# Last expert stage of a decoder block on one core: four result buffers, a first expert by single chunks, and three drains of GpSimd

## The chip, the cores and the metric

The program runs on one core of one Trainium2 chip. The metric is the device time of one execution, in microseconds. The core has five engines with instruction streams of their own: TensorE (PE; its weight loads are PEld), VectorE (DVE), ScalarE (ACT), GpSimd (POOL) and SyncE (SP), and 16 DMA engines. Engines wait for each other by semaphores; each executes its own stream in order.

## The reference

Two gated residual pairs over x of 32 x 128 tokens with 256 columns, all in float32:

```python
x = x + tanh(g_xattn[0]) * _L0_xattn_ref(_layernorm(x), ctx, ctx, mask, ...)  # 16 heads of 16
x = x + tanh(g_ffn[0])   * _L0_ffn_ref(_layernorm(x), ...)    # 8 experts, each takes its best 512 tokens
x = x + tanh(g_xattn[1]) * _L1_xattn_ref(_layernorm(x), ctx, ...)
x = x + tanh(g_ffn[1])   * _L1_ffn_ref(_layernorm(x), wg, W, b)
```

The change is mostly in the last line, a feed-forward in which each token goes to its first choice of 8 experts, and each expert takes its first 512 tokens:

```python
probs = softmax(xt @ wg); idx = argmax(probs)
mask = one_hot(idx, 8); locations = cumsum(mask, axis=0) - mask
mask = mask * (locations < 512)
gate = sum(probs * mask)
exp_out = einsum('ech,efh->ecf', exp_in, W) + b[:, None, :]
out = einsum('tec,ecf->tf', gate * dispatch, exp_out)
```

## The kernel before

The program has two blocks, each closed by a barrier of all engines: the front (layer norm and attention of the first pair) and `behind_attention` (L2262 on), in which five stages stand one behind the other in each engine's stream: routing, expert choice, the second attention (`bidirectional_stage`, L1504), and the last expert stage (`first_choice_stage`, L2117). Semaphores alone order the stages, so an engine that has finished its part of one begins with the next. On leaving the program a context clears all semaphores and passes a second barrier (L48, L49).

GpSimd issues all indirect DMAs, each of 128 rows: 32 that gather rows for expert choice (L1357), 32 that add its results (L1366), 32 that scatter the rows of the second attention into `slots` (L1651), ordered by expert, and 32 that scatter the results of the last stage into the output (L2161).

In the second attention's stream on GpSimd (`on_gpsimd`, loop over steps s from -2 to 10, L1643) a step has the inverse deviation of quad s - 2 of the result, the four slot scatters of quad s - 3, and the inverse deviation of the input of quad s + 2. A quad is 4 tiles of 128 tokens; there are 8. The last two steps with work give GpSimd eight scatters without a pause between them.

The last stage works expert by expert (8), each of 512 slots in four chunks of 128:

- SyncE (`on_sync`, L2144) waits for all 32 slot scatters, and then loads expert 0's rows in two halves (L2151) and those of experts 1 to 3 whole (L2153). The weights of experts 0 to 3 were loaded earlier. Weights, bias and rows of expert e from 4 on are loaded when all results of expert e - 4 are there (L2136).
- VectorE (`on_vector`) has `norm(e)`, four instructions that normalise an expert's chunks into `xn` (L2183); `index(e)`, which makes the target indices `idx` (L2189) and from expert 2 on waits until the scatters of expert e - 2 have landed, since `y` and `idx` have two buffers each (L2188); `chunk(e, c)`, bias (L2197) and gated residual (L2192) of one chunk; and `pair(e, j)`, bias of two chunks in one instruction (L2203) and two results. Its order is norm 0, index 0, norm 1, chunks 0 and 1 of expert 0, norm 2, pair (0, 1), index 1, pair (1, 0), norm 3, pair (1, 1), index 2, and so on.
- TensorE (`on_tensor`) turns two chunks at a time (`turn`, four transposes by the identity, L2231) and multiplies them by the weights (`pair`, eight matmuls, L2245), two matmuls a chunk.
- ScalarE copies each turned pair from PSUM to `rT` (L2173).
- GpSimd (`on_gpsimd`, L2155) waits for the stores of the attention, then issues for each expert four scatters, each behind its result (L2160), and at the end waits until all have landed (L2165).

The order of VectorE's stream is written out by hand:

```python
        norm(0)
        index(0)
        norm(1)
        for e in range(EXPERTS):
            if e == 0:
                chunk(0, 0)
                chunk(0, 1)
            else:
                pair(e, 0)
            if e + 2 < EXPERTS:
                norm(e + 2)
            pair(e, 1)
            if e + 1 < EXPERTS:
                index(e + 1)
```

## Time and profile before

| | |
|---|---|
| median of 3 runs | 802.15 us (800.67 to 803.16) |
| the profiled execution | 800.73 us |
| its span, first to last instruction | 798.9 us |
| mean granted clock of TensorE | 0.936 of full speed |
| busy: PE, DVE, ACT, POOL | 85%, 54%, 39%, 33% |

Times in a trace are microseconds from the start of the span; those marked ns are nanoseconds. In a timeline a row is a run of like instructions: start, length, engine, line, operation, output<-inputs, shapes, count, and in brackets the engine's idle time before it with what ended it. `POOLq`, `SPq` and the like are instructions of an engine's sequencer, such as a DRAIN or a wait for a semaphore. Ends of matmuls are modelled. The granted clock is given as a share of TensorE's full speed: 1.00 is 2.4 GHz, 0.50 is 1.2 GHz. A scatter's instruction on GpSimd ends when the DMA has been issued, not when it has landed.

### The profile page before, as it was taken

The numbers are of one execution on the slowest core, as the hardware profiler recorded it, in microseconds if no ns is written. First come the engines' busy times: TensorE is split into PE (matmuls) and PEld (weight loads), VectorE is DVE, ScalarE is ACT, GpSimd is POOL, SyncE is SP. The second block draws the span as 40 slices with busy tenths as digits, with TensorE's granted clock in tenths as the row PEclk, the third lists the DMA queues.
The fourth block names the chain that finished last, engine by engine and source line by source line (L and its number), as shares of the span: only waits on it lengthen the run. The fifth ranks groups of instructions, "written<-read, shape, count | busy, mean of one in ns | idle before, by whom it ended". The sixth has DMA issues, their size and how long they took to land.

```text
span 798.9 us, 14703 instructions
## 1 busy us (share of the span) xinstructions
PE 675.1 (85%) x5289; PEld 462.4 (58%) x5289; DVE 433.6 (54%) x1317; ACT 315.1 (39%) x673; POOL 260.3 (33%) x377
## 2 busy tenths in 40 slices
PE   5999998999999975847999999995799999982980
PEld 3565655555555543623666666664677778761860
DVE  5645546777787746782222222103567776772781
ACT  2343434777777762532222222222554444301220
POOL 4101102244334422005555555221113332224563
PEclk9999997999999997966999999997899999996995
DMA  8569924466676118912363893216233451113651
GB/s 269 186 180 253 257 101 96 91 135 135 129 132 128 57 55 200 171 40 83 50 155 48 256 260 75 47 21 196 80 106 133 140 179 50 59 53 129 208 168 53
DMA packets 105039, 103.10 MB, mean 129 GB/s; under 512 B 22102, under 2 KB 95321, under 8 KB 104964
## 3 DMA queue, kind: packets, MB, share of 16 engines
q1 hardware_dynamic: 95752, 85.72, 41.2%
q0 software_dynamic: 9216, 16.46, 9.2%
q8 instruction: 42, 0.69, 0.4%
q14 instruction: 29, 0.24, 0.1%
HBM read 60.15 MB, written 42.25 MB: 128 GB/s over the span
## 4 chain that ended last, share of the span: by engine, by line
PE 35%; DVE 7%; issue 6%; ACT 4%; POOL 4%; DMA 3%; another core or an unknown queue 1%; SPq 0%; POOLq 0%; DVEq 0%; ACTq 0%
PE pc L1486 9%; PE pc L1463 9%; PE pc L950 3%; POOL result L2161 2%; PE pc L2029 2%; ACT enc L1851 2%; PE pc L1991 1%; PE pc L1988 1%; PE pc L1482 1%; PE pc L2051 1%; DVE d_w_c L1772 1%; PE pc L1466 1%; PE pc L1959 1%; PE pc L1450 1%
## 5 line engine op out<-in xcount | busy, mean ns | idle before, releaser
L617 ACT ACTIVATE probs<-pb,b_key_cols 128x512 f32<-128x512 f32 x128 | 92.7, 779 | 16.6 <-PE pb L787 16.6
L484 DVE TENSOR_REDUCE neg_max<-pb 128x4 f32<-128x512 f32 x128 | 81.7, 680 | 3.5 <-PE pb L767 3.5
L1366 POOL DMA_INDIRECT scratch_resid<-y,k_idx x32 | 54.7, 1708 | 87.3 <-DVE y L1416 87.0
L1463 PE MATMUL pc<-gT,w_up 128*128 128x512 f32 x160 | 72.6, 610 | 0.9 <-DVE gT L1398 0.9
L1486 PE MATMUL pc<-w_dn,mid 128*128 128x256 f32 x320 | 73.3, 384 | 0.0
L1434 ACT ACTIVATE mid<-pc,b_up 128x512 f32<-128x512 f32 x40 | 27.5, 687 | 113.4 <-PE pc L1463 111.4
L1486 PEld LDWEIGHTS pc<-w_dn,mid 128*128 128x128 f32 x320 | 59.5, 190 | 12.7 <-issue 5.3
L1463 PEld LDWEIGHTS pc<-gT,w_up 128*128 128x128 f32 x160 | 31.3, 196 | 37.7 <-issue 37.3
L1416 DVE TENSOR_SCALAR y<-pc,gate 128x256 f32<-128x256 f32 x32 | 15.5, 484 | 65.7 <-PE pc L1486 47.9
L1357 POOL DMA_INDIRECT rows<-scratch_rows,k_idx x32 | 31.1, 973 | 56.8 <-DVE k_idx L1240 47.4
L365 POOL CAST nm_parts<-neg_max 128x16 bf16<-128x16 f32 x32 | 6.3, 196 | 124.9 <-DVE neg_max L484 124.9
L800 PE MATMUL pb<-probs,v_wide 128*32 128x128 f32 x1024 | 42.5, 285 | 1.8 <-ACT probs L617 1.8
L863 PE MATMUL pb<-wo,attnT 128*128 128x264 f32 x128 | 37.6, 417 | 5.1 <-ACT attnT L664 0.9
L1398 DVE COPY gT<-pc 128x512 f32<-128x512 f32 x8 | 5.5, 692 | 65.9 <-PE pc L1450 65.1
L2161 POOL DMA_INDIRECT result<-g_y,g_idx x32 | 31.8, 992 | 24.5 <-DVE g_y L2192 14.5
L502 DVE SCALAR_TENSOR_TENSOR s_x<-pb,s_tanh_g,s_x 128x264 f32<-128x264 f32 x32 | 15.8, 493 | 41.7 <-PE pb L863 41.7
L1651 POOL DMA_INDIRECT scratch_slots<-s_x,r_dest x32 | 32.5, 1016 | 9.4 <-issue 9.4
L1991 PE MATMUL pc<-d_w_c,encT 128*128 128x256 f32 x128 | 33.9, 388 | 0.0
L1988 PE MATMUL pc<-k_w_f,ehqT 128*128 128x256 f32 x128 | 33.5, 385 | 0.0
L787 PE MATMUL pb<-qs,ks 51*128 51x128 bf16 x512 | 26.0, 223 | 8.4 <-ACT probs L617 8.4
L691 PE MATMUL pb<-cT,wk 128*128 128x512 f32 x64 | 32.1, 645 | 1.3 <-ACT cT L584 1.3
L1639 POOL TENSOR_TENSOR d_vareps<-d_moments,s_eps 128x4 f32<-128x4 f32 x8 | 1.6, 197 | 94.0 <-DVE d_moments L1735 94.0
(336 smaller groups left out, 1443.1 us busy)
## 6 DMA issues: line engine op xcount, KB each, us to landing
qs<-scratch_qparts SPq DMA_DIRECT2D x48, 128.0 KB, 4.3
ks<-scratch_kparts SPq DMA_DIRECT2D x48, 128.0 KB
w_dn<-in_W_down SPq DMA_DIRECT2D x8, 640.0 KB
scratch_slots<-s_zero SPq DMA_DIRECT2D x1, 4160.0 KB, 19.1
c_in<-in_ctx SPq DMA_DIRECT2D x8, 512.0 KB, 6.5
s_x<-in_x SPq DMA_DIRECT2D x8, 512.0 KB, 7.0
scratch_ctxT<-cT SPq DMA_DIRECT2D x8, 512.0 KB, 6.5
scratch_resid<-s_x SPq DMA_DIRECT2D x16, 256.0 KB, 3.1
```

The lines of the kernel that those rows point to most:

```text
L484: V.tensor_reduce(neg_max[:, h:h + 4], ps_s[b][:].rearrange("p (h k) -> p h k", h=4), AX.X, ALU.max, negate=True).then_inc(max_s, 1)
L617: A.activation(probs[2 * u + b][:], ps_st[b][:].rearrange("p (h q) -> p h q", h=4), ACT.Exp, bias=key_cols[:, 1, t:t + 1], scale=key_cols[ ...
L691: ins = M.matmul(ps_ck[m][:], wk[:, h, m * P:(m + 1) * P], cT[q % 2][:, h, :], start=(h == 0), stop=(h == HALVES - 1))
L800: ins = M.matmul(ps_ctx[32 * j:32 * j + SLOTW, g * P:(g + 1) * P], v_wide[t % 2][:, 4 * g + j, :], probs[2 * u + b][:, j, :], start=True, ...
L863: ins = M.matmul(ps_o, attnT[:, h, :], wo[:, h, :], start=(h == 0), stop=(h == HALVES - 1))
L1366: pool.indirect_dma_start(out=T["resid"], out_offset=bass.IndirectOffsetOnAxis(ap=S["idx"][:, e, c:c + 1], axis=0), in_=y[e % 2][:, c, :], ...
L1463: ins = nc.tensor.matmul(ps_u[k % 4][:], w, gT[e % 2][:, h, :], start=(h == 0), stop=(h == HALVES - 1))
L1486: ins = nc.tensor.matmul(here(c), mid[e % 2][m][:, c * P:(c + 1) * P], w_dn[e % 2][:, m, :], start=False, stop=(m == MT - 2))
L1651: pool.indirect_dma_start(out=T["slots"], out_offset=bass.IndirectOffsetOnAxis(ap=dest[:, t, :], axis=0), in_=rows[:, t, :], in_offset=Non ...
L1988: M.matmul(here, ehqT[q % 2][:, h, cols], w_f[:, 2, h, :], start=False, stop=False)
L1991: ins = M.matmul(here, encT[q % 2][:, h, cols], w_c[q % 2][:, t, h, :], start=False, stop=(h == HALVES - 1))
L2161: pool.indirect_dma_start(out=T["out"], out_offset=bass.IndirectOffsetOnAxis(ap=idx[e % 2][:, c:c + 1], axis=0), in_=y[e % 2][:, c, :], in ...
```

## The change

In the second attention GpSimd gets a `drain()` at step 1. In the last stage:

- `y`, `idx` and the semaphores `sent` have four buffers instead of two, and `index(e)` waits for scatters from expert 4 on, for those of expert e - 4.
- Expert 0's rows are loaded as chunk 0 and then chunks 1 to 3. It is turned, copied and multiplied chunk by chunk, each chunk in a PSUM bank of its own. VectorE's order becomes norm 0, index 0, chunks 0 and 1, norm 1, chunks 2 and 3, norm 2, index 1, and then from expert 1 on as before.
- TensorE waits for all slot scatters and turns the identity 14 times ahead of chunk 0.
- GpSimd drains at the start of the stage and once behind the last scatter, ahead of the waits for the landings.

```diff
--- before.py
+++ after.py
@@ -1653,6 +1653,8 @@
                                             bounds_check=TOKENS - 1, oob_is_err=False).then_inc(sent_s, 16)
             if is_quad(s + 2):
                 inverse_deviation(s + 2)
+            if s == 1:
+                pool.drain()
 
     def tables_on_vector(dve):
         V = nc.vector
@@ -2116,16 +2118,18 @@
 
 def first_choice_stage(nc, S, T, sem, sb, ps, bidir):
 
-    ST = CAP // P
+    ST, WARM = CAP // P, 14
     two = lambda n, s, d=F32: [sb(f"{n}{i}", s, d) for i in range(2)]
     rows, xn = [sb(f"g_rows{i}", [P, ST, ROW1]) for i in range(4)], [sb(f"g_xn{i}", [P, ST, D]) for i in range(3)]
     rT = two("g_rT", [P, HALVES, CAP])
     w, bias = S["w_1"], S["b_1"]
-    yb, y, idx = two("g_yb", [P, ST, D]), two("g_y", [P, ST, D]), two("g_idx", [P, ST], I32)
-    sent = [sem(f"pg_sent{i}") for i in range(2)]
+    yb = two("g_yb", [P, ST, D])
+    y, idx = [sb(f"g_y{i}", [P, ST, D]) for i in range(4)], [sb(f"g_idx{i}", [P, ST], I32) for i in range(4)]
+    sent = [sem(f"pg_sent{i}") for i in range(4)]
     in_s = [sem(f"pg_in{i}") for i in range(4)]
-    half_s = sem("pg_half")
-    place = lambda e, c: ps[6 if (e, c) == (0, 1) else 4 + e % 2 * 2 + c // 2][:, c % 2 * D:(c % 2 + 1) * D]
+    rest_s = sem("pg_rest")
+    place = lambda e, c: ps[(4, 6, 5, 7)[c] if e == 0 else 4 + e % 2 * 2 + c // 2][:, c % 2 * D:(c % 2 + 1) * D]
+    turned = lambda e, j: ST + 2 * (e - 1) + j + 1
     xn_s, t_ps, rT_s, y_ps, yb_s, y_s, idx_s = (sem("pg_" + n) for n in ("xn", "t_ps", "rT", "y_ps", "yb", "y", "idx"))
     slots_t = T["slots"].rearrange("(c p) d -> p c d", p=P)
 
@@ -2147,27 +2151,33 @@
             if e >= 4:
                 weights(sp, e)
             if e == 0:
-                for j in range(2):
-                    sp.dma_start(rows[0][:, 2 * j:2 * j + 2, :], slots_t[:, 2 * j:2 * j + 2, :]).then_inc((in_s[0], half_s)[j], 16)
+                sp.dma_start(rows[0][:, 0:1, :], slots_t[:, 0:1, :]).then_inc(in_s[0], 16)
+                sp.dma_start(rows[0][:, 1:ST, :], slots_t[:, 1:ST, :]).then_inc(rest_s, 16)
             else:
                 sp.dma_start(rows[e % 4][:], slots_t[:, e * ST:(e + 1) * ST, :]).then_inc(in_s[e % 4], 16)
 
     def on_gpsimd(pool):
+        pool.drain()
         pool.wait_ge(bidir.stored_s, 16 * QUADS)
         for e in range(EXPERTS):
             pool.wait_ge(idx_s, e + 1)
             for c in range(ST):
                 pool.wait_ge(y_s, e * ST + c + 1)
-                pool.indirect_dma_start(out=T["out"], out_offset=bass.IndirectOffsetOnAxis(ap=idx[e % 2][:, c:c + 1], axis=0),
-                                        in_=y[e % 2][:, c, :], in_offset=None,
-                                        bounds_check=TOKENS - 1, oob_is_err=False).then_inc(sent[e % 2], 16)
-        for par in range(2):
-            pool.wait_ge(sent[par], 16 * ST * EXPERTS // 2)
+                pool.indirect_dma_start(out=T["out"], out_offset=bass.IndirectOffsetOnAxis(ap=idx[e % 4][:, c:c + 1], axis=0),
+                                        in_=y[e % 4][:, c, :], in_offset=None,
+                                        bounds_check=TOKENS - 1, oob_is_err=False).then_inc(sent[e % 4], 16)
+        pool.drain()
+        for i in range(4):
+            pool.wait_ge(sent[i], 16 * ST * EXPERTS // 4)
 
     def on_scalar(act):
-        for e in range(EXPERTS):
+        for c in range(ST):
+            act.wait_ge(t_ps, c + 1)
+            nc.scalar.activation(rT[0][:, :, c * P:(c + 1) * P], ps[c][:, 0:D].rearrange("p (h t) -> p h t", h=HALVES),
+                                 ACT.Copy).then_inc(rT_s, 1)
+        for e in range(1, EXPERTS):
             for j in range(2):
-                act.wait_ge(t_ps, 2 * e + j + 1)
+                act.wait_ge(t_ps, turned(e, j))
                 if e >= 2:
                     act.wait_ge(y_ps, (e - 2) * ST + 2 * j + 2)
                 nc.scalar.activation(rT[e % 2][:, :, 2 * j * P:2 * (j + 1) * P], ps[e % 2 * 2 + j][:].rearrange("p (h t) -> p h t", h=HALVES),
@@ -2176,20 +2186,21 @@
     def on_vector(dve):
         def norm(e):
             if e >= 3:
-                dve.wait_ge(t_ps, 2 * (e - 2))
+                dve.wait_ge(t_ps, ST if e == 3 else turned(e - 3, 1))
+            dve.wait_ge(in_s[e % 4], 48 * (e // 4 + 1))
             for c in range(ST):
-                if c % 2 == 0:
-                    dve.wait_ge(half_s if e == 0 and c else in_s[e % 4], 16 if e == 0 and c else 48 * (e // 4 + 1))
+                if (e, c) == (0, 1):
+                    dve.wait_ge(rest_s, 16)
                 nc.vector.tensor_scalar(xn[e % 3][:, c, :], rows[e % 4][:, c, 0:D], rows[e % 4][:, c, D:D + 1], rows[e % 4][:, c, D + 1:D + 2],
                                         ALU.subtract, ALU.mult).then_inc(xn_s, 1)
 
         def index(e):
-            if e >= 2:
-                dve.wait_ge(sent[e % 2], 16 * (e // 2) * ST)
-            nc.vector.tensor_scalar(idx[e % 2][:], rows[e % 4][:, :, D + 3], -1.0, float(TOKENS), ALU.mult, ALU.add).then_inc(idx_s, 1)
+            if e >= 4:
+                dve.wait_ge(sent[e % 4], 16 * (e // 4) * ST)
+            nc.vector.tensor_scalar(idx[e % 4][:], rows[e % 4][:, :, D + 3], -1.0, float(TOKENS), ALU.mult, ALU.add).then_inc(idx_s, 1)
 
         def result(e, c):
-            nc.vector.scalar_tensor_tensor(y[e % 2][:, c, :], yb[e % 2][:, c, :], rows[e % 4][:, c, D + 2:D + 3],
+            nc.vector.scalar_tensor_tensor(y[e % 4][:, c, :], yb[e % 2][:, c, :], rows[e % 4][:, c, D + 2:D + 3],
                                            rows[e % 4][:, c, 0:D], ALU.mult, ALU.add).then_inc(y_s, 1)
 
         def chunk(e, c):
@@ -2208,13 +2219,15 @@
 
         norm(0)
         index(0)
+        chunk(0, 0)
+        chunk(0, 1)
         norm(1)
-        for e in range(EXPERTS):
-            if e == 0:
-                chunk(0, 0)
-                chunk(0, 1)
-            else:
-                pair(e, 0)
+        chunk(0, 2)
+        chunk(0, 3)
+        norm(2)
+        index(1)
+        for e in range(1, EXPERTS):
+            pair(e, 0)
             if e + 2 < EXPERTS:
                 norm(e + 2)
             pair(e, 1)
@@ -2222,10 +2235,27 @@
                 index(e + 1)
 
     def on_tensor(pe):
+        def turn_chunk(c):
+            pe.wait_ge(xn_s, c + 1)
+            for h in range(HALVES):
+                ins = nc.tensor.transpose(ps[c][:, h * P:(h + 1) * P], xn[0][:, c, h * P:(h + 1) * P], S["ident"][:])
+            ins.then_inc(t_ps, 1)
+
+        def product(e, c):
+            for h in range(HALVES):
+                ins = nc.tensor.matmul(place(e, c), rT[e % 2][:, h, c * P:(c + 1) * P],
+                                       w[e % 4][:, h, :], start=(h == 0), stop=(h == HALVES - 1))
+            ins.then_inc(y_ps, 1)
+
+        def product_of_first(c):
+            pe.wait_ge(rT_s, c + 1)
+            if c == 0:
+                pe.wait_ge(in_s[0], 48)
+            product(0, c)
+
         def turn(e, j):
             pe.wait_ge(xn_s, e * ST + 2 * j + 2)
-            if e >= 2:
-                pe.wait_ge(rT_s, 2 * (e - 2) + j + 1)
+            pe.wait_ge(rT_s, 2 + j + 1 if e == 1 else 2 * j + 2 if e == 2 else turned(e - 2, j))
             for h in range(HALVES):
                 for c in (2 * j, 2 * j + 1):
                     ins = nc.tensor.transpose(ps[e % 2 * 2 + j][:, (2 * h + c % 2) * P:(2 * h + c % 2 + 1) * P], xn[e % 3][:, c, h * P:(h + 1) * P],
@@ -2233,22 +2263,30 @@
             ins.then_inc(t_ps, 1)
 
         def pair(e, j):
-            pe.wait_ge(rT_s, 2 * e + j + 1)
+            pe.wait_ge(rT_s, turned(e, j))
             if j == 0:
                 pe.wait_ge(in_s[e % 4], 48 * (e // 4 + 1))
             if e >= 2:
                 pe.wait_ge(yb_s, (e - 2) * ST + 2 * j + 2)
-            if (e, j) == (1, 0):
-                pe.wait_ge(yb_s, 2)
+            if e == 1:
+                pe.wait_ge(yb_s, 2 * j + 2)
             for c in (2 * j, 2 * j + 1):
-                for h in range(HALVES):
-                    ins = nc.tensor.matmul(place(e, c), rT[e % 2][:, h, c * P:(c + 1) * P],
-                                           w[e % 4][:, h, :], start=(h == 0), stop=(h == HALVES - 1))
-                ins.then_inc(y_ps, 1)
-
-        turn(0, 0)
-        turn(0, 1)
-        for e in range(EXPERTS):
+                product(e, c)
+
+        pe.wait_ge(bidir.sent_s, 16 * TILES)
+        for _ in range(WARM):
+            nc.tensor.transpose(ps[7][:, 0:P], S["ident"][:], S["ident"][:])
+        turn_chunk(0)
+        turn_chunk(1)
+        product_of_first(0)
+        turn_chunk(2)
+        product_of_first(1)
+        turn_chunk(3)
+        product_of_first(2)
+        turn(1, 0)
+        product_of_first(3)
+        turn(1, 1)
+        for e in range(1, EXPERTS):
             pair(e, 0)
             if e + 1 < EXPERTS:
                 turn(e + 1, 0)
```

## Rows read from the trace of the kernel before

**Rows 1.** The page: chain by line, and two groups (busy us, mean ns, idle).
```profile
PE pc L1486 9%; PE pc L1463 9%; PE pc L950 3%; POOL result L2161 2%; PE pc L2029 2%; ACT enc L1851 2%; PE pc L1991 1%; PE pc L1988 1%; PE pc L1482 1%; PE pc L2051 1%; DVE d_w_c L1772 1%; PE pc L1466 1%; PE pc L1959 1%; PE pc L1450 1%
...
L1366 POOL DMA_INDIRECT scratch_resid<-y,k_idx x32 | 54.7, 1708 | 87.3 <-DVE y L1416 87.0
...
L1357 POOL DMA_INDIRECT rows<-scratch_rows,k_idx x32 | 31.1, 973 | 56.8 <-DVE k_idx L1240 47.4
```

**Rows 2.** Line 2161's instructions (ns min/median/max, first to last start), and who waited.
```profile
L2161 POOL DMA_INDIRECT result<-g_y,g_idx x32: 971/973/1142, 742.8 to 787.4; - x32
...
  DVE g_idx L2189: 7.7, 5
```

**Rows 3.** Timeline of POOL, last stage.
```profile
744.09 0.97 POOL L2161 DMA_INDIRECT result<-g_y,g_idx  x1 [0.30 <-issue]
746.13 0.97 POOL L2161 DMA_INDIRECT result<-g_y,g_idx  x1 [1.07 <-DVE g_y L2192]
...
752.70 0.97 POOL L2161 DMA_INDIRECT result<-g_y,g_idx  x1 [0.31 <-issue]
754.74 1.03 POOL L2161 DMA_INDIRECT result<-g_y,g_idx  x1 [1.06 <-issue]
...
773.10 1.03 POOL L2161 DMA_INDIRECT result<-g_y,g_idx  x1 [0.67 <-issue]
```

**Rows 4.** Timeline of DVE, in expert 2.
```profile
752.67 0.69 DVE L2203 TENSOR_TENSOR g_yb<-pc,b 128x512 f32<-128x512 f32 x1
...
754.19 1.38 DVE L2183 TENSOR_SCALAR g_xn<-g_rows 128x256 f32<-128x256 f32 x4
```

**Rows 5.** Timeline of all engines, head of the last stage.
```profile
733.48 0.88 SPq L2151 DMA_DIRECT2D g_rows<-scratch_slots  x2
...
736.16 1.46 DVE L2183 TENSOR_SCALAR g_xn<-g_rows 128x256 f32<-128x256 f32 x4 [9.67 <-DMA g_rows<-scratch_slots]
...
736.95 1.97 PE L2231 MATMUL pc<-s_ident,g_xn 128*128 128x128 f32 x8 [12.09 <-DVE g_xn L2183]
...
739.65 1.38 DVE L2183 TENSOR_SCALAR g_xn<-g_rows 128x256 f32<-128x256 f32 x4 [1.95 <-DMA g_rows<-scratch_slots]
740.94 0.42 DVE L2197 TENSOR_TENSOR g_yb<-pc,b 128x256 f32<-128x256 f32 x1
741.40 0.48 DVE L2192 SCALAR_TENSOR_TENSOR g_y<-g_yb,g_rows 128x256 f32<-128x256 f32 x1
```

**Rows 6.** Instructions of lines 2165 and 2264, tail of the program.
```profile
L2165 POOLq EVENT_SEMAPHORE  x1: 17/17/17, 789.8 to 789.8; - x1
...
L2264 POOLq DRAIN  x1: 7162/7162/7162, 790.0 to 790.0; - x1
```

**Rows 7.** Instructions of lines 49 and 48, POOL's other drains.
```profile
L49 POOLq DRAIN  x2: 45/46/46, 305.9 to 798.6; - x2
...
L48 POOLq DRAIN  x2: 184/235/286, 305.2 to 797.4; - x2
```

**Rows 8.** Timeline of POOL, second attention.
```profile
593.14 0.20 POOL L1639 TENSOR_TENSOR d_vareps<-d_moments,s_eps 128x4 f32<-128x4 f32 x1 [13.81 <-DVE d_moments L1735]
```

**Rows 9.** Instructions of line 1651.
```profile
L1651 POOL DMA_INDIRECT scratch_slots<-s_x,r_dest x32: 971/976/1283, 612.5 to 731.1; - x32
```

**Rows 10.** Lines 2231 and 2245, from 736.9 to 740.6 us and from 742 to 750.
```profile
L2231 PE MATMUL pc<-s_ident,g_xn x8: 421/421/476, 737.0 to 738.5; 128*128 128x128 f32 x8
...
L2245 PE MATMUL pc<-w,g_rT x4: 634/634/793, 738.8 to 740.2; 128*128 128x256 f32 x4
...
L2245 PE MATMUL pc<-w,g_rT x31: 379/379/382, 742.1 to 749.9; 128*128 128x256 f32 x31
```

**Rows 11.** Groups by form, an ACT copy of 256 columns.
```profile
L664 ACT ACTIVATE attnT<-pb 128x256 f32<-128x256 f32 x32 | 12.3, 383 | 39.3 <-PE pb L891 39.3
```

**Rows 12.** Windows: stretch, length, busy of PE, PEld, DVE, ACT, POOL, then PEclk.
```profile
736.95:740.93 3.98, 3.98 (x13) 3.38 (x14) 2.03 (x7) 1.19 (x2) 0.00 (x0) 0.50 1.02 341
740.94:752.70 11.76, 11.76 (x67) 10.33 (x67) 9.24 (x25) 2.99 (x5) 7.00 (x7) 1.00 0.54 157
```

## The prediction

> **What bounds the kernel now.** I read the page first, for its chain of waits and its groups; then GpSimd's instructions and timeline in the last stage; then the two ends of that stage, because the edits sit there. The page's chain is spread thinly over many lines, with GpSimd's result scatters (L2161) the only line of the last stage in it [rows 1]. Their own view says why: 32 scatters, the first starts at 742.8 and the last at 787.4 [rows 2]. Where they are queued, from 773.10 to 787.4, eleven steps take 14.3 us, 1.30 each [rows 2, 3]. 31 such steps would be 40.3 us and the stage takes 44.6, so 4.3 us are holes. They have two kinds: at the start (744.09 to 746.13, one step too long by 0.7) and about once per expert later (752.70 to 754.74) [rows 3]. The view of the line names the second kind: VectorE's index waited 7.7 us, in five pieces, for landed scatters [rows 2], which is the wait for one of two result buffers. Without it VectorE would need 1.52 us for a pair (752.67 to 754.19), 1.38 for normalising, 1.52 for the second pair and under 0.2 for the index, 4.6 an expert [rows 4], against 4 x 1.30 = 5.2 on GpSimd. So the stage's floor is GpSimd issuing, once it is fed.
>
> At the head of the stage SyncE issues the loads at 733.48, and VectorE waits until 739.65 to normalise expert 1 before it takes expert 0's first product at 740.94 [rows 5]. At the tail the last scatter starts at 787.4, its landing is seen at 789.8, and then one DRAIN of GpSimd takes 7.16 us, from 790.0 [rows 2, 6]. Everything after it is 798.9 less 797.2, 1.7 us.
>
> **The drains.** GpSimd's drains of two other lines took 0.05 to 0.29 us, at 305 behind the front part and at 797 right behind the long one [rows 7]. The long one differs in what preceded it: 128 indirect DMAs (four groups of 32, at L1357, L1366, L1651 and L2161) since the drains at 305, none before the short ones [rows 1, 2, 9]. All had landed, so it isn't a wait for data. I read it as settling something per DMA: 7.16 / 128 = 0.056 us each. The trace doesn't show a drain after fewer DMAs; its bounds are 0.05 (a drain after none) and 7.16 (after all), and by the backlog of 32 DMAs I take 1.8.
> - Drain at s == 1: it stands behind GpSimd's work for quad 3; the next instruction is at 593.14, after 13.8 us of idle time [rows 8]. 64 DMAs make 3.6 us, even 7.16 fits. Queued behind it is only that next instruction, so it costs nothing.
> - Drain at the start of the last stage: GpSimd's last slots scatter starts at 731.1 and takes 1.0 [rows 9], its next work comes at about 740 (below). 32 DMAs, 1.8 us; 7.16 would end at 739.3, still hidden. Waiting behind it would be the first result scatter.
> - Drain behind the last scatter: it starts 1.0 after that scatter's start and ends at 2.8; the landing comes at 2.4 and hides all but 0.4. Then 0.24 as now from landing to drain, the last drain at about 0.2, and 1.7: 4.9 us from the last start to the end, where it is 798.9 - 787.4 = 11.5 now. **Saved: 6.6.** Ends: 7.0 if the third is short (the landing then decides), 1.2 if it takes 7.16 itself, 0 if the last keeps its 7.16.
>
> Now a rule against this. The row shows 7162 ns [rows 6]. The Trainium skill, page "VectorE: DVE Perf Modes", section "The DRAIN you can't avoid", says of the drains that frame a kernel that they are a constant of about 12 ns on all five engines. By it neither an early nor a late drain could be worth anything; this trace doesn't agree: even GpSimd's shortest take 45 ns, and I go by the row.
>
> **The head of the stage.** SyncE now loads chunk 0 alone (a quarter instead of a half) and the other three together. Today the half reaches VectorE 2.68 us after the issue at 733.48 [rows 5]; the bytes halved are worth at most that share of it that is transfer, and I take 0.35: VectorE at 735.8, its first 0.41 us done at 736.2. The rest lands as the second half does now, about 736.9. TensorE runs 14 turned identities from 733.5 on. At the lower clock turns start 0.21 apart ((1.97 - 0.42) / 7 = 0.22 at most) and last 0.42 [rows 5, 10], so they end at 736.5: they hold chunk 0's turns back 0.3 us. Then: turns of chunk 0 to 737.15; ScalarE's copy of 256 columns, 0.38 us by a like copy [rows 11], to 737.6; TensorE turns chunk 1 meanwhile (its normalised rows are there at 737.3) to 737.8; product of chunk 0.
> What clock has that product? Now it is 0.50 until 740.93, four microseconds after TensorE began at 736.95 [rows 12]. It will have begun at 733.5 and be nearly unbroken, so I put the rise at about 737.5. Two matmuls then take 0.6 (379 ns, 0.22 apart) instead of 1.1 (634 ns, 0.43 apart) [rows 10]: product at 738.3, or 738.9 if the clock stays low.
> VectorE: rest of expert 0 normalised and index by 738.05; chunk 0 at 738.3, 0.94 for bias and result (740.94 to 741.88) [rows 5]; GpSimd 0.9 later, at **740.1** instead of 742.8. Chunk 1 follows to 740.15 (expert 1's rows are in at 739.65 as now); normalising expert 1 to 741.4; chunks 2 and 3, results at 742.35 and 743.25; normalising expert 2 (now behind all chunks of expert 0) to 744.5; index; pair (1,0), results at 745.8 and 746.2; normalising expert 3, pair (1,1) first result at 748.65. GpSimd, 1.30 a step or result plus 0.85: 740.1, 741.4, 743.2, 744.5, then a hole, 746.65, 747.95, 749.5 for the seventh. From there VectorE (4.6) outruns GpSimd (5.2). Four buffers make the index of expert e wait for scatters of e - 4, which VectorE's lead of at most 4 us never reaches, so no hole comes back. Loads of experts 4 to 7 are let go by the results of four experts before, a little earlier than now; they are needed over 6 us later, and the first load took 2.7. TensorE does 24 instructions an expert and did 67 in the 11.76 us of the stretch in which it never paused [rows 12], 4.2 us an expert, less than 5.2.
> Last scatter: 749.5 + 25 x 1.30 = 782.0. **Saved: 5.4** of 787.4. With the low clock until 741 every step is 0.6 to 1 us later: 4.4. Ends: 3.0 if, beside the low clock, a later landing of chunk 1 and VectorE's work before pair (1,0) make the holes 1.4 longer, and 7.6 with no hole at all (740.1 + 31 x 1.28 = 779.8).
>
> **Sum.** 5.4 + 6.6 = 12.0: span 786.9. The profiled execution took 800.73 (span 798.9), the median of the runs is 802.15; I take the difference off the median: **790.2 us**.
>
> **Rivals.** A difference of 0.3%, 2.4 us, is about what a measurement of this kernel can tell from none.
> - *The clock stays low until 741* (TensorE pauses about 0.4 us before chunk 1): 5.4 becomes 4.4, 791.2. For it: the rise came late before as well. Against: hardly a gap is left. Chance 0.14.
> - *A drain costs 7.16 whenever any indirect DMA stands before it.* The first two stay hidden, the third doesn't: 1.2 instead of 6.6, 795.6. For it: no trace shows a middle value. Against: 7.16 is odd as a flat fee beside 0.05. 0.08.
> - *The 7.16 belong to the end of the block, whatever was drained earlier.* Then the change's drains don't do what they should: 802.15 - 5.4 = 796.8. This is also where the page's rule would leave it, with drains of no weight in themselves; the rows give it little, 0.07.
> - *Slower: a drain with transfers in flight waits far longer than one that finds all landed.* The second and third drains both stand right behind scatters. At price D the second holds GpSimd until 732.1 + D, and 31 steps lead to 772.4 + D; the third adds D again: the span ends at 775.5 + 2D. It decides from D = 11.7 us on; with D = 14.3 (twice the 7.16) the span is 804.1, the time 807.4. Against: the scatters land 1.4 us after their end. 0.03.
>
> **How the numbers follow.** Forecast 0.62 (790.2); the four rivals 0.32; 0.06 for a mixture that leaves about no gain or something not seen. The low end is the forecast with no hole at the head, 802.15 - 14.2 = 788.0; the high end takes in the flat fee, 796.0. Left out are the third rival (0.07), the slower one (0.03), most of the 0.06 and a little below the low end: about 0.2. Faster by over 0.3%: 0.62 + 0.14 + 0.08 + 0.07 and a little, 0.92; within 0.3%: 0.05; slower 0.03.
>
> **What would show it.** Drains of GpSimd of about 3.6, 1.8, 1.8 and 0.2 us; the first result scatter at about 740; one hole before the fifth, none of over 0.3 us after the seventh; no wait of VectorE for a landed scatter; the clock at 1.0 from about 737.5. Wrong it would be by a third drain near 7 us, a last drain near 7 us, a first scatter after 741.5, or steps between scatters of over 1.35 on average.

## The result, and the profile after

The changed kernel took 798.33 us (median of 8 runs, 795.73 to 800.41), the kernel before 801.2 us beside it (8 runs, 800.19 to 805.91): ratio 0.995, 95% interval 0.993 to 0.9971. It is faster, by 2.9 us between the medians where 12.0 were forecast; 798.3 lies outside the forecast range of 788 to 796. The profiled execution took 796.69 us, its span is 794.9 us (before 800.73 and 798.9), the mean granted clock 0.944 (0.936).

The page of the changed kernel, the group of the result scatters:

```profile
L2166 POOL DMA_INDIRECT result<-g_y,g_idx x32 | 32.1, 1002 | 26.1 <-DVE g_y L2203 19.0
```

The same line by its instructions (ns min/median/max, first to last start; then what ended its idle time):

```profile
L2166 POOL DMA_INDIRECT result<-g_y,g_idx x32: 972/976/1202, 740.8 to 789.0; - x32
its engine sat idle before it (us, times) until:
  DVE g_y L2203: 19.0, 9
  issue: 7.2, 23
```

Beside [rows 2]: the first scatter comes 2.0 us earlier (740.8, was 742.8), the last 1.6 us *later* (789.0, was 787.4). No wait of the index for landed scatters is left. So the last stage lost more than its head won; what remains of the gain is behind the last scatter: 794.9 - 789.0 = 5.9 us, where it was 11.5. The new drains, and the one that closes the block (views of four lines, the same columns):

```profile
L1657 POOLq DRAIN  x1: 6470/6470/6470, 577.8 to 577.8; - x1
...
L2160 POOLq DRAIN  x1: 6223/6223/6223, 728.4 to 728.4; - x1
...
L2169 POOLq DRAIN  x1: 5069/5069/5069, 787.7 to 787.7; - x1
...
L2302 POOLq DRAIN  x1: 55/55/55, 793.1 to 793.1; - x1
```

A drain's record here begins while the scatters ahead of it are still being issued (the third at 787.7, the last scatter at 789.0), so its length says little; its end does. The third ends at 787.70 + 5.07 = 792.77, 2.8 us after the last issue's end (789.99). The one that cost 7.16 us in [rows 6] takes 0.055.

The timeline of the head, beside [rows 5]:

```profile
733.28 3.25 PE L2278 MATMUL pc<-s_ident 128*128 128x128 f32 x14 [8.65 <-DMA scratch_slots<-s_x,r_dest]
...
735.47 0.41 DVE L2194 TENSOR_SCALAR g_xn<-g_rows 128x256 f32<-128x256 f32 x1 [9.22 <-DMA g_rows<-scratch_slots]
...
737.00 0.38 ACT L2176 ACTIVATE g_rT<-pc 128x256 f32<-128x256 f32 x1 [13.47 <-PE pc L2241]
737.11 1.06 DVE L2194 TENSOR_SCALAR g_xn<-g_rows 128x256 f32<-128x256 f32 x3 [1.23 <-DMA g_rows<-scratch_slots]
...
737.85 1.03 PE L2246 MATMUL pc<-w,g_rT 128*128 128x256 f32 x4
...
738.92 0.42 DVE L2208 TENSOR_TENSOR g_yb<-pc,b 128x256 f32<-128x256 f32 x1 [0.67 <-PE pc L2246]
...
740.80 0.99 POOL L2166 DMA_INDIRECT result<-g_y,g_idx  x1 [8.97 <-DVE g_y L2203]
```

Windows of the same kernel (columns as in [rows 12]):

```profile
733.28:736.40 3.12, 3.12 (x15) 3.12 (x16) 0.41 (x1) 0.00 (x0) 0.00 (x0) 0.50 0.66 163
737.06:751.00 13.94, 12.82 (x71) 11.05 (x72) 12.71 (x35) 4.46 (x9) 6.83 (x7) 1.00 0.69 220
```

The head is what was forecast, clock included. A chunk's product is two matmuls in the code and four in the profile, 1.03 us. The stage goes wrong later. The timeline of all engines in experts 3 and 4:

```profile
753.84 0.60 PE L2261 MATMUL pc<-s_ident,g_xn 128*128 128x128 f32 x4
...
754.28 1.89 PE L2246 MATMUL pc<-w,g_rT 128*128 128x256 f32 x8
...
756.01 0.60 PE L2261 MATMUL pc<-s_ident,g_xn 128*128 128x128 f32 x4
...
758.28 0.60 ACT L2183 ACTIVATE g_rT<-pc 128x512 f32<-128x512 f32 x1 [5.37 <-remote]
758.93 1.59 PEld L2246 LDWEIGHTS pc<-w,g_rT 128*128 128x128 f32 x8 [2.56 <-issue]
...
759.35 0.97 POOL L2166 DMA_INDIRECT result<-g_y,g_idx  x1 [0.31 <-issue]
...
761.91 0.69 DVE L2214 TENSOR_TENSOR g_yb<-pc,b 128x512 f32<-128x512 f32 x1 [4.02 <-PE pc L2246]
...
763.92 0.97 POOL L2166 DMA_INDIRECT result<-g_y,g_idx  x1 [3.59 <-DVE g_y L2203]
```

TensorE's turns for expert 4 are recorded at 753.84 and over by 754.44. ScalarE, which waits for them (and for a product of expert 2 that VectorE had read long before), copies them at 758.28. The product for the second half of expert 3 is recorded at 754.28 and over by 756.17; VectorE, idle for 4.0 us, takes it at 761.91, and GpSimd, which needs the result, has a hole of 3.6 us. These are two late completions of TensorE beside each other: the product did not wait for the late copy. A second hole, of 3.1 us, lies before the scatter at 782.45. A lower clock did not cause them: windows of one microsecond show 1.00 from 751 to 781. It fell to 0.50 at the end of the second hole, ahead of the last product. In the view of waits, from 730 us on, the same shows as waits ended by "remote", for which the trace has no recorded instruction that ended them:

```profile
POOL result L2166 <- DVE g_y L2203: 19.0, 9, 9.0
ACT g_rT L2183 <- remote: 15.7, 3, 5.4
...
ACT g_rT L2183 <- PE pc L2261: 10.9, 6, 3.0
...
DVE g_yb L2214 <- remote: 5.9, 1, 5.9
```

(columns: engine and line, what it waited for, us in total, times, longest). I call it "late completions of TensorE" below. The word "remote" marks only part of them: the wait of 4.0 us above is put down to TensorE. The kernel before has it too, and I had not read it: its waits from 740 to 800 us hold

```profile
ACT g_rT L2173 <- remote: 7.8, 3, 3.2
```

### The profile page after: what moved, and what is told of

Same layout as the page of the kernel before. It is cut to its first block, busy times and chain, and to the rows that moved or that the text cites. A ratio compares the mean times of both kernels' runs of the same rounds, so it can differ in the third digit from the quotient of the medians.

```text
span 794.9 us, 14740 instructions
## 1 busy us (share of the span) xinstructions
PE 676.6 (85%) x5303; PEld 464.4 (58%) x5303; DVE 433.9 (55%) x1318; ACT 315.6 (40%) x675; POOL 261.0 (33%) x377
## 4 chain that ended last, share of the span: by engine, by line
PE 38%; DVE 9%; issue 4%; ACT 4%; DMA 3%; another core or an unknown queue 2%; POOL 1%; POOLq 0%; SPq 0%; DVEq 0%; ACTq 0%
PE pc L1486 9%; PE pc L1463 9%; PE pc L950 3%; PE pc L2246 2%; PE pc L2031 2%; PE pc L1990 1%; ACT enc L1853 1%; PE pc L1993 1%; PE pc L1482 1%; DVE d_w_c L1774 1%; PE pc L2053 1%; PE pc L1466 1%; DVE d_stats L1745 1%; PE pc L1450 1%
## 5 line engine op out<-in xcount | busy, mean ns | idle before, releaser
L1366 POOL DMA_INDIRECT scratch_resid<-y,k_idx x32 | 54.7, 1709 | 87.0 <-DVE y L1416 86.7
L2246 PE MATMUL pc<-w,g_rT 128*128 128x256 f32 x128 | 32.5, 396 | 9.6 <-ACT g_rT L2183 4.9
```

The source lines that it names most:

```text
L1366: pool.indirect_dma_start(out=T["resid"], out_offset=bass.IndirectOffsetOnAxis(ap=S["idx"][:, e, c:c + 1], axis=0), in_=y[e % 2][:, c, :], ...
L2246: ins = nc.tensor.matmul(place(e, c), rT[e % 2][:, h, c * P:(c + 1) * P], w[e % 4][:, h, :], start=(h == 0), stop=(h == HALVES - 1))
```

## The experiments

Eighteen runs of eleven kernels follow. The kernel before took 791.3 us beside the first four; beside all others 801.7 to 805.8 (801.2 beside the timing above), in one case on the very chip that had given 791.3. No run shows what differed. I call them the short and the long condition. Each ratio is to the kernel before beside it.

### The two parts alone, short condition

drains_only is the kernel before with the three drains; no_drains is the changed kernel without them.

```diff
+            if s == 1:
+                pool.drain()
...
     def on_gpsimd(pool):
+        pool.drain()
...
+        pool.drain()
         for par in range(2):
```

> The kernel before with the three drains alone. Theory A (the drains carry the whole gain, the rest of the change nothing): the last scatter starts where it does before, about 787.4, and the tail behind it shrinks from 11.5 to about 5.9 us as in the changed kernel, so about 795.6 us, ratio 0.993. Theory B (the drains and the head of the stage both gain, and something else took 6 us back by chance of that run): the same tail, but the changed kernel is then clearly faster than this one. The third drain should take about 2.8 us from the end of the last scatter's instruction.

> The changed kernel without its three drains, so with the four buffers, the single chunks and the turned identities alone. Theory A (late completions of TensorE eat what the head and the buffers bring): last scatter between 786 and 790, one last drain of about 7 us, 800 to 804 us. Theory B (they bring what was forecast, 5.4 us, and the profiled execution was unlucky): 795 to 797 us.

drains_only: ratio 0.9923 (0.9897 to 0.9949), about 6.1 us of 791.3, 5.8 us from the last scatter to the end. no_drains: 0.9954 (0.9935 to 0.9972), 3.6 us. From SyncE's load of the rows to the last scatter, which is free of what comes earlier, drains_only takes 776.7 - 723.0 = 53.7 us and no_drains 774.3 - 724.2 = 50.1: also 3.6. The stage without drains:

```profile
L2163 POOL DMA_INDIRECT result<-g_y,g_idx x32: 972/975/1212, 731.7 to 774.3; - x32
```

One hole ahead of the fifth scatter and no other, no wait ended by "remote" in the stage, and a turned pair reaches ScalarE at once (744.79 + 0.60 = 745.39):

```profile
744.79 0.60 PE L2257 MATMUL pc<-s_ident,g_xn 128*128 128x128 f32 x4
...
745.42 0.60 ACT L2179 ACTIVATE g_rT<-pc 128x512 f32<-128x512 f32 x1 [1.57 <-PE pc L2257]
```

So in the short condition both parts work: together 9.7 us by the two ratios, if they add (the whole was not timed there), where 12.0 were forecast. The times expected for these two runs were for the long condition and can't be compared.

### The same in the long condition

after_again, after_third and after_fourth are the changed kernel, before_again the kernel before, drains_only_again and no_drains_again the kernels above. For after_third, too, 0.992 to 0.995 was expected where the kernel before takes about 802 us.

> The changed kernel once more, now beside its parts. The kernel before took 791 us where the parts were run and 801 where the changed kernel was first timed, and only in the first traces do TensorE's completions arrive late (up to 6 us). Theory A (the late completions belong to the chip or its condition, and cost the changed kernel more than the one before, because its last stage leans on TensorE without a pause): where the kernel before takes about 791, this one is at 0.987 to 0.989 of it, with the last scatter 50 us behind the first load and no lag above 0.5 us; where the kernel before takes about 801, it is at 0.995 again with two holes of about 3 us. Theory B (the parts don't add up anywhere): 0.992 to 0.995 in either place.

> The kernel before, for its trace in the same place as the trace of the changed kernel. Theory A: at a time of about 791 its trace has no lag of TensorE's completions, and last scatter starts 53 to 54 us behind the first load; at about 801 it has lags in the second attention and in the last stage.

> The kernel before with the three drains alone, beside the changed kernel. Theory A: at 802 the two are equal within 1 us, since the late completions take back what the head and the buffers give; at 791 the changed kernel is faster by 3 to 4 us. Theory B: equal in both places.

> The changed kernel without the three drains, that is the head and the four buffers alone. It had 0.9954 where the kernel before takes 791 us. Where the kernel before takes some 802 us: Theory A, the unbroken issuing gives back what head and buffers gain: two holes of 3 to 5 us, 47 to 49 us from first to last scatter, ratio 0.998 to 1.002. Theory B, head and buffers gain their part wherever they run, and the drains are worth less there: ratio 0.994 to 0.997.

| kernel | ratio (95%) | first scatter to last, us | rows' load to last scatter |
|---|---|---|---|
| before, the two profiles | | 44.6, 45.6 | 53.9, 55.7 |
| after_again | 0.9924 (0.9897 to 0.9951) | 49.1 | 56.6 |
| after_third | 0.994 (0.9921 to 0.9959) | 48.7 | 56.1 |
| after_fourth | 0.9922 (0.9894 to 0.995) | 47.1 | 54.7 |
| drains_only_again | 0.9934 (0.9909 to 0.996) | 45.4 | 55.2 |
| no_drains_again | 1.0 (0.9979 to 1.0021) | 49.1 | 57.1 |
| no_third_drain (below) | 0.9929 (0.9906 to 0.9952) | 46.4 | 53.9 |
| no_first_drain (below) | 0.9939 (0.9918 to 0.996) | 47.5 | 55.1 |

As far as these times can tell, the drains are the whole gain: 0.9934 alone, and 0.9934 is also the mean of the changed kernel's four ratios (0.995, 0.9924, 0.994, 0.9922; the first timing was its worst). Head and buffers alone give nothing, within 1.7 us either way, where the short condition had 3.6. All kernels of the table with the head reach their first scatter 7.5 to 8.0 us after the load, the kernel before after 9.3 and 10.1. In this condition all nine profiles with four buffers and no pauses have two steps of 2.9 to 5.0 us; the five in which the index still waits for landings (head_two_waits below among them) have none or one, of up to 4.3. So two buffers have holes too, but fewer. before_again has late completions too (two waits of ScalarE ended by "remote", 8.1 us) and one step of 4.3.

Where the long condition begins shows in no_drains and no_drains_again, the same kernel on the same chip. Their first slots scatters start at 613.1 and 613.6 us, their last ones at 721.8 and 730.8: 8.5 of the 16.0 us between the two spans arise in the second attention, 7.1 in the last stage.

### What a drain costs

no_third_drain is the changed kernel without the drain behind the last scatter, no_first_drain without the one at s == 1.

> The changed kernel without its third drain alone. Theory C (a drain first waits for the landing, about 1.4 us behind the end of the last issue, and then settles each indirect DMA since the drain before at 0.043 us): the last drain, from behind the landing, takes 1.4 us, and the time is that of the changed kernel within 0.3 us: the third drain hides nothing. Theory D (a drain settles at 0.08 us a DMA from the end of the last issue on, beside the landing): the last drain takes 2.6 to 2.8 us and the kernel is 1.2 us slower.

> The changed kernel without the drain at step 1 of the second attention, so that the one at the start of the last stage finds 96 indirect DMAs instead of 32. It ends 2.75 us after the last issue in the changed kernel. By a price per DMA it ends 6.8 to 8.1 us after the last issue, at or after the first result scatter is due (8.9 us after it), so the time stays within 0.3 us; by a flat price it stays at 2.75.

The drain lines of no_drains, no_third_drain, no_first_drain and no_scatter (below), in this order:

```profile
L2298 POOLq DRAIN  x1: 7162/7162/7162, 777.0 to 777.0; - x1
```

```profile
L2301 POOLq DRAIN  x1: 2660/2660/2660, 792.1 to 792.1; - x1
```

```profile
L2158 POOLq DRAIN  x1: 9707/9707/9707, 731.8 to 731.8; - x1
```

```profile
L2171 POOLq DRAIN  x1: 4642/4642/4642, 765.6 to 765.6; - x1
```

The first two stand behind the landed data and so show the price pure: 7.16 us after 128 indirect DMAs, 2.66 after 32. The third stands behind 96 and ends 6.2 us after the last slots scatter's issue (735.29 to 741.53), the fourth behind 8, 1.8 us after the last issue (768.40 to 770.20). The drain at s == 1 in the changed kernel, behind 64, ends 5.3 us after GpSimd's last instruction. 8, 32, 64, 96, 128 DMAs: 1.8, 2.7, 5.3, 6.2, 7.2 us. It grows with the DMAs since the last drain, but not at 0.056 each. Two expectations missed here: 8 were expected to take under 1 us, and 96 from 6.8 to 8.1 us. The 64 are gathers and additions, the 8 and 32 are scatters; whether the kind counts beside the number, no run tells.

no_third_drain: 0.9929 (0.9906 to 0.9952), 7.1 us from last scatter to end instead of 5.9: the drain beside the landing hides 1.2 us, and the other two do most of the work. no_first_drain: 0.9939 (0.9918 to 0.996); its drain of 96 ends 2.8 us before the first result scatter (744.31) and is still hidden. By the ratios neither can be told from the whole change.

### Issuing, or moving rows?

no_scatter leaves out the result scatters of experts 1 to 6; out_of_range gives those experts indices beyond the output, so that GpSimd issues them and no row is moved. In no_scatter the waits for the scatters that are left out go too. Each ran once in either condition.

```diff
                 pool.wait_ge(y_s, e * ST + c + 1)
+                if 1 <= e <= 6:
+                    continue
```

```diff
-... -1.0, float(TOKENS), ALU.mult, ALU.add)
+... -1.0, float(TOKENS if e in (0, 7) else 3 * TOKENS), ALU.mult, ALU.add)
```

> The changed kernel, with the scatters of experts 1 to 6 left out (their rows don't reach the output). Theory A (TensorE's completions arrive late because GpSimd issues scatters without a pause): no lag of a completion above 0.5 us in the last stage, and VectorE finishes expert 7 at about 776 to 778, set by TensorE and VectorE's 4.3 to 4.6 us an expert. Theory B (TensorE's completions are late whatever GpSimd does): two delays of 3 to 6 us stay, at about 755 to 762 and 775 to 781. The last drain, after 8 DMAs, should be under 1 us by a price per DMA.

> The changed kernel, with the target indices of experts 1 to 6 out of range, so that GpSimd issues all 32 scatters but 24 of them move no rows (those rows are not written). If the issuing itself makes TensorE's completions late, the holes of 3 us stay as in the changed kernel, last scatter near 789. If the data that the scatters move make them late, they are gone, and the last scatter starts near 782 to 783.

> The changed kernel, with the scatters of experts 1 to 6 left out (their rows don't reach the output). At 802: if GpSimd's scatters make TensorE's completions late (theory P), the lags in the second attention stay, where its scatters are still issued, and those of the last stage are gone, with the first of the remaining scatters of expert 7 at 32 to 33 us behind that of expert 0, as it was at 791. If TensorE is late by itself in its busiest stretches (theory T), lags of 1 us and more stay in the last stage and this distance is 36 us or more.

> The changed kernel, with the target indices of experts 1 to 6 out of range, so that 24 of 32 scatters move no rows (those rows are not written). At 802: if the moving of rows makes the completions late, no lag in the last stage and about 42.6 us from the first to the last scatter, as it was at 791; if the issuing does, or TensorE itself, lags of over 1 us stay and the distance is 47 us or more.

Short condition: 774.28 and 779.74 us; out_of_range takes 42.7 us from first to last scatter, as no_drains does with its rows moved (42.6). Without the scatters expert 7's first comes 32.7 us after expert 0's first: 32.7 / 7 = 4.7 us an expert, by my estimate what VectorE needs, under the 4 x 1.32 of GpSimd. Long condition: 779.97 and 797.21 us. The waits from 740 to 780 us, first without the scatters, then with scatters that move nothing:

```profile
POOL result L2168 <- DVE g_y L2205: 28.4, 2, 28.1
ACT g_rT L2185 <- PE pc L2263: 17.6, 11, 1.8
ACT g_rT L2185 <- PE pc L2248: 1.6, 1, 1.6
```

```profile
ACT g_rT L2183 <- PE pc L2261: 18.6, 8, 4.7
POOL result L2166 <- DVE g_y L2203: 15.3, 7, 8.9
...
ACT g_rT L2183 <- remote: 6.5, 1, 6.5
...
DVE g_yb L2214 <- remote: 4.2, 1, 4.2
```

Without scatters no completion is late in the last stage, and it takes 33.6 us instead of 32.7. With issued but empty ones they are late, and the holes are steps of 4.4 and 5.0 us. In the second attention, where both kernels issue the slots scatters, both keep theirs, and in the short condition there are none at all. So in the last stage the lateness goes with GpSimd issuing scatters, not with rows moved; this rests on one profile of each kernel. Issuing alone is not enough: in the expert choice, from 358 to 540 us, GpSimd issues 64 indirect DMAs, 32 of them gathers and 32 additions, and none of the 20 profiles has a wait ended by "remote" before its first slots scatter. In all 16 of the long condition the first such wait ends 3.5 to 4.2 us after that scatter's start (615.63 against 612.10 in the changed kernel's profile).

### Which part opens the holes?

head_two_waits keeps the change but makes the index of expert e wait for the scatters of e - 2, as with two buffers. drains_buffers is the kernel before with the drains and four buffers and its old head. pool_pause is the changed kernel with a memset on GpSimd behind each of the first seven experts.

```diff
         def index(e):
-            if e >= 4:
-                dve.wait_ge(sent[e % 4], 16 * (e // 4) * ST)
+            if e >= 2:
+                dve.wait_ge(sent[(e - 2) % 4], 16 * ((e - 2) // 4 + 1) * ST)
```

```diff
+    pause = sb("g_pause", [P, EXPERTS - 1, 1024])
...
+            if e < EXPERTS - 1:
+                nc.gpsimd.memset(pause[:, e, :], 0.0)
```

> The changed kernel once more, beside the three variants below. The theory that both parts of the change add (0.9923 for the drains and 0.9954 for the head and buffers, where the kernel before took 791 us) has, where the kernel before takes some 791 us, 0.986 to 0.990 and no hole of over 2 us between two scatters. Where the kernel before takes some 802 us both theories have 0.992 to 0.995, with the scatters of the stage 48 to 49 us from first to last and two holes of 3 to 5 us.

> The changed kernel with its own head and four buffers, but the indices of expert e (from 2 on) wait until the scatters of expert e-2 have landed, as with two buffers before. Theory A, GpSimd's unbroken issuing is what makes TensorE's completions late and opens the holes: where the kernel before takes some 802 us the two holes of 3 to 5 us are gone or under 2 us, first to last scatter takes 45 to 46 us instead of 48 to 49, and the ratio to the kernel before is 0.988 to 0.992. Theory B, the lateness comes with the number of scatters whatever their pace, and the holes come from the head or the place of the turned halves: the holes stay and the ratio is 0.993 to 0.996. Where the kernel before takes some 791 us there are no late completions, and the returned waits cost 0 to 3 us against the changed kernel.

> The kernel before with the three drains and four result and index buffers, but its old head by pairs (two halves of 256 rows, one buffer of turned rows' banks as before). Theory A, the lost waits on landed scatters are what opens the holes: where the kernel before takes some 802 us first to last scatter is 47 to 49 us (45.4 with the drains alone), the last scatter is no earlier than with the drains alone, ratio 0.992 to 0.996. Theory B, the new head is to blame: 43 to 45 us, and the ratio falls to 0.985 to 0.989. Where the kernel before takes some 791 us the buffers alone give 1 to 2 us beside the drains: ratio 0.990 to 0.992.

> The changed kernel with one memset of 128x1024 on GpSimd, about 0.9 us by the 1.8 us of a 128x2048, after the scatters of each of the first seven experts: 6.3 us of GpSimd's time added, and nothing else. Theory A: where the kernel before takes some 802 us the holes shrink by about what the pauses take, so the last scatter is no more than 2 us later than in the changed kernel, and may be earlier. Theory B, GpSimd's pace has nothing to do with it: the last scatter is some 4 to 6 us later than in the changed kernel, ratio 0.999 to 1.002. Where the kernel before takes some 791 us the pauses cost all of the 6 us that no wait of GpSimd covers: 3 to 6 us.

> The changed kernel with index(e) waiting for the landed scatters of expert e-2, once more. Theory A: first to last scatter 45 to 46 us where the kernel before takes some 802 us, no hole over 2.5 us, and over both tries a ratio no worse than the changed kernel's 0.992 to 0.994. If it beats the changed kernel at all it is by under 0.3%, which a single comparison can't tell. Where the kernel before takes 791 us: 43 to 45 us, ratio 0.988 to 0.991.

drains_buffers (0.9951, 0.9926 to 0.9976): 48.4 us from first to last scatter, 59.1 from the load, the longest of all; with the old head, the drains and two buffers it was 45.4 and 55.2. Of the difference from the load 0.8 lies ahead of the first scatter. Its timeline of GpSimd has both holes:

```profile
761.80 0.98 POOL L2165 DMA_INDIRECT result<-g_y,g_idx  x1 [0.30 <-issue]
766.19 1.04 POOL L2165 DMA_INDIRECT result<-g_y,g_idx  x1 [3.42 <-DVE g_y L2197]
...
780.81 0.97 POOL L2165 DMA_INDIRECT result<-g_y,g_idx  x1 [0.30 <-issue]
785.71 0.97 POOL L2165 DMA_INDIRECT result<-g_y,g_idx  x1 [3.93 <-DVE g_y L2197]
```

So the holes come with the buffers, without the new head too. The times don't settle it: 0.9951 and 0.9934 lie within each other's intervals. head_two_waits: 0.9923 (0.9898 to 0.9947) and again 0.9918 (0.9896 to 0.9939); 45.0 and 46.1 us, 53.0 and 53.5 from the load, 1.2 to 3.6 less than the changed kernel's four profiles. The first of the two profiles is of the fastest of its six executions (794.39, median 798.37), so it flatters; and no_third_drain, with two holes, had 46.4 and 53.9. The first try has no step over 2.3 us, the second one of 3.6, so my "no hole over 2.5" missed there. Its waits for landings came back,

```profile
  DVE g_y L2203: 13.1, 5
  issue: 9.9, 27
...
  DVE g_idx L2200: 4.8, 3
```

and by the times they cost as much as the holes they prevent: 0.9923 against 0.9922 for the changed kernel beside it. pool_pause: 0.9924 (0.99 to 0.9948), beside the same 0.9922.

```profile
766.52 1.00 POOL L2167 DMA_INDIRECT result<-g_y,g_idx  x1 [0.30 <-issue]
767.51 0.97 POOL L2171 MEMSET g_pause<- 128x1024 f32 x1
768.65 0.97 POOL L2167 DMA_INDIRECT result<-g_y,g_idx  x1 [0.17 <-DVE g_y L2206]
```

A step with a memset takes 2.13 instead of 1.28 us, 0.85 more. The first of the seven falls into the hole ahead of the fifth scatter, a step of 2.2 with and without it; the other six add some 5 us. No wait in this stage is ended by "remote" and no step is longer than 2.3 us: 47.9 us from first to last scatter, where the changed kernel has 47.1 to 49.1. Five microseconds of added work on the engine that sets the pace cost nothing that these times can tell (their intervals are 2 us either way).

The clock was not as steady as the head needs: in pool_pause it was still at its lower level during the first products,

```profile
736.90:741.00 4.10, 3.42 (x12) 2.56 (x11) 1.52 (x5) 0.77 (x2) 0.00 (x0) 0.50 1.08 366
```

a chunk's product took 1.91 us instead of 1.03, and the first scatter came 8.7 us after the load instead of 7.5: my rival of the late clock, in one profile of the new head. In two more (head_two_waits, no_drains_again) the first product took 1.4 us and the first scatter came after 8.0. TensorE's wait for chunk 1 does not sort them: 0.68 us in pool_pause, 0.62 in the changed kernel's profile, where the clock had risen at 737.06, and 0.74 in no_first_drain, whose first product took 1.03.

## Why the prediction was wrong

**The drains: right in kind, sized 1 us off.** The reading that the 7.16 us settle the indirect DMAs since the last drain holds, and both rivals on a flat fee fall: the closing drain fell to 0.055. The term failed at 0.056 us each: the drain of 32 takes 2.7, not 1.8, the tail 5.9, not 4.9, and saves 5.6, not 6.6. The first two are hidden, as said. Against it I had set the Trainium skill, page "VectorE: DVE Perf Modes", section "The DRAIN you can't avoid", which gives the drains that frame a kernel as a constant of about 12 ns on all five engines. That does not hold for GpSimd's drains behind indirect DMAs, the closing one of the block among them: here 1.8 to 7.2 us.

**The head: nearly right.** The load, the 14 turns, the clock at about 737.5 (737.06) and the hole before the fifth scatter came as said. The first scatter stands 7.5 us behind the load, 6.6 forecast; 0.4 to 0.5 of the 0.9 is one slip: "Two matmuls then take 0.6" took two matmuls of the code for two of the profile's. [rows 10] show four for chunk 0 (x4, 738.8 to 740.2), and in the changed kernel four take 1.03 us. Steps of 1.32 instead of 1.30 add 0.5 over 25. With both the sum would have been some 4 us, and the short condition shows 3.6.

**The step that failed: "from there VectorE outruns GpSimd", "so no hole comes back".** I costed TensorE at 4.2 us an expert from a stretch in which it never paused, and so by what it issues, not by when others learn of it. Of the 7.0 us between the forecast last scatter (782.0) and the real one (789.0), 0.8 is there by the seventh (750.26 against 749.5) and 6.2 come behind it, 6.1 of them in two steps of 4.6 and 4.1 us where 1.3 is usual. In the rows of the kernel before, ScalarE already waited 7.8 us for completions ended by "remote", and the sum has no term for it. The buffers were costed as a pure gain: they take away VectorE's 7.7 us of waiting for landings [rows 2]. The runs show the price: in the long condition the kernels without these waits have two large steps each, which give back what buffers and head together gain (no_drains_again, 1.0). In the short condition the step holds: one hole, no late completion, 3.6 us gained. The sum of 12.0 was wrong by 7.0 in the stage (5.4 saved were forecast, 1.6 were lost) and by 1.0 at the drains: 5.6 saved at the tail, less the 1.6, are the 4.0 between the two spans. The repeats gained more than the first timing, 4.8 to 6.3 us by their ratios, still far from 12.0.

What is shown, by traces and mostly by one of each kernel: in the last stage the lateness goes with issuing (no_scatter_again against out_of_range_again), and the second hole with the buffers (nine profiles against five). That pauses on GpSimd remove or shrink the holes rests on three profiles, and no time confirms it. What stays open is why the two engines meet at all, what differs between the short and the long condition, and whether TensorE executes when its record says and is heard late, or executes later than its record says. No run here tells these apart.

No version beat the changed kernel by more than the runs can tell. head_two_waits has the best two profiles in the long condition (spans 792.6 and 793.3 against 794.2 to 796.1), and its ratios, 0.9923 and 0.9918, lie inside the changed kernel's 0.9922 to 0.995.

## What to carry to other kernels

Drain GpSimd where it idles anyway: the price of the closing drain is that of the indirect DMAs since the last one, and the drain behind 64 of them at s == 1 ended about 8.5 us before GpSimd's next work. Before you price an engine by what it issues, look in the waits of its consumers for ones ended by something that is not its record; such waits here (7.8 us in the kernel before) were a sign that GpSimd might not be the stage's only floor. And taking away a wait for a buffer need not be a gain: measure the buffers without the rest of the change.

## What the runs showed of the hardware that I had not expected

- A GpSimd drain costs 1.8, 2.7, 5.3, 6.2 and 7.2 us behind 8, 32, 64, 96 and 128 indirect DMAs. Behind 32 it is 2.7 when all have landed and 2.8, counted from the last issue, when they have not. With 24 of the 32 scatters moving no rows, out_of_range's third drain ends 2.7 us after the last issue.
- In the long condition TensorE's completions reached ScalarE 3.8 us and VectorE 5.7 us behind the recorded end while GpSimd issued indirect scatters; other profiles have waits of ScalarE of up to 7.1 us, where 1.6 is usual. It happens in the last stage and in the second attention, where VectorE's wait for them in the changed kernel is

```profile
DVE s_x L1728 <- remote: 12.4, 5, 3.4
```

- The same program on the same chip (no_drains) had none of this and took 788.2 us at one time, and had it and took 803.4 at another; the kernel before took 791.3 and 802.4 beside it.
